# An LSTM expert kernel: state halves exchanged by label, so that one half alone takes the input

## The chip, the cores and the metric

The kernel runs on one core of a Trainium2 chip, as one program. The metric is the device time of an execution in microseconds. Before the change it is 1760.58 us, the median of 3 runs (1759.59 to 1762.61).

## The reference, cut to what matters

A token sequence of 16 x 512 goes through an embedding with a short-time spectrum, local attention, and a layer of eight LSTM experts of which each token takes two. The experts' layer is this (from the reference, cut):

```
logits = flat_x @ router_w + router_b
top_vals, top_idx = jax.lax.top_k(logits, K)
rw = jax.nn.softmax(top_vals, axis=1)
mask = (top_idx.T[:, None, :] == jnp.arange(E)[None, :, None]).astype(x.dtype)
expert_x = (mask[..., None] * flat_x[None, None]).reshape(K, E, S_, B_, I_)
...
gates = xt @ Wi + h @ Wh + b
i_, f_, g_, o_ = jnp.split(gates, 4, axis=-1)
c = jax.nn.sigmoid(f_) * c + jax.nn.sigmoid(i_) * jnp.tanh(g_)
h = jax.nn.sigmoid(o_) * jnp.tanh(c)
...
y = jnp.einsum('ken,nk,keno->no', mask, rw, out)
```

E is 8 experts, K is 2 choices. The scan runs over 16 steps, with 512 columns (sequence positions) in each. For each choice k and expert e there is a state of its own (h and c, 128 x 512), which goes on in every step; its input is x where the k-th choice is e, and zero elsewhere. So an expert has two states, 128 x 1024 together, and at most one of the two gets an input at a given column, since the two choices of a token differ.

## The kernel before, in words

All tensors have the 128 features on the partitions and the columns along the free dimension. The program is written out for five engines by hand, with semaphores. The unit of time in the code is t, from 0 to 31 in a step: t = 4 e + g, with the expert e (a unit) and the gate g in the order I, G, F, O. Each engine's function `step(s, ...)` walks over t and issues what belongs there. `run_front` issues beside it the front of the next step (embedding, norms, attention, choice of experts), each piece at the t that the tables PE_AT, ACT_AT, DVE_AT and SP_AT give for it; pieces for the step after begin at t = 24. Nothing is reordered at run time: an instruction that waits holds its engine's queue.

One unit, on each engine:

- TensorE, `unit_gate` (line 551): for each gate, twelve f16 products of 512 columns into one of two PSUM slots. An f32 operand is held as two f16 parts, HI and LO; three products (HI HI, HI LO, LO HI) stand for one. There are two halves k (the two choices), and an input and a recurrent part: 3 x 2 x 2. Gate n waits until the tanh of gate n-2 has emptied its slot. At g = 0 also `unit_y` (L557), one f32 product of the chosen state of unit e-2 with wo.
- Scalar: `gate_tanh` (L713, 1024 columns) for each gate into `tmp`, `cell_tanh` (L720) at g = 3, `split_hi` (L724, the HI part of h of the unit before) at g = 0.
- VectorE: `hidden` of the unit before at g = 0 (L1051); at g = 1 `masked_input` of the next unit (L1044, both halves, both parts), `hidden_lo` (L1056) and `input_part` (L1066); at g = 2 `chosen` of the unit before (L1087 selects the half that the token chose, L1091 multiplies by the weight) and `cell` (L1072, L1076). Step 0 has no gate F and L1063 in place of L1066.
- SyncE loads masks for unit e+2 at g = 1 and the weight rows at g = 3, each broadcast to 128 partitions from a small DRAM tensor.

Pieces of the front that the prediction names: L841 one-hot rows, L463 embedding, L851 and L981 variance, L857 normalisation (first at t = 29, second at t = 19), L1163 root on GpSimd, L470 and L643 transpose and copy xnT (t = 30), L475 the q, k, v products (t = 31), L490 window scores, L502 values (t = 15), L516 transposes of the second normalised input (t = 20), L817 residuals of the weights ahead of step 0.

## Time and profile before

| | before |
|---|---|
| median of 3 runs | 1760.58 us |
| profiled execution | 1761.26 us |
| its span | 1759.5 us |
| TensorE busy (matmul) | 1692.6 us, 96% |
| VectorE busy | 1543.5 us, 88% |
| Scalar busy | 1000.6 us, 57% |
| GpSimd busy | 48.8 us, 3% |
| granted TensorE clock, mean | 0.986 of full speed |

The span is the time from the first to the last instruction of the profiled execution. The first 90 us hold the set-up and the first front; steps of some 106 us follow. Times in the rows are counted from the span's start.

### The profile page before, as it was taken

The numbers are of one execution on the slowest core, as the hardware profiler recorded it, in microseconds if no ns is written. First come the engines' busy times: TensorE is split into PE (matmuls) and PEld (weight loads), VectorE is DVE, ScalarE is ACT, GpSimd is POOL, SyncE is SP. The second block draws the span as 40 slices with busy tenths as digits, with TensorE's granted clock in tenths as the row PEclk, the third lists the DMA queues.
The fourth block names the chain that finished last, engine by engine and source line by source line (L and its number), as shares of the span: only waits on it lengthen the run. The fifth ranks groups of instructions, "written<-read, shape, count | busy, mean of one in ns | idle before, by whom it ended". The sixth has DMA issues, their size and how long they took to land.

```text
span 1759.5 us, 25844 instructions
## 1 busy us (share of the span) xinstructions
PE 1692.6 (96%) x9864; PEld 822.0 (47%) x9864; DVE 1543.5 (88%) x2419; ACT 1000.6 (57%) x1124; POOL 48.8 (3%) x42
## 2 busy tenths in 40 slices
PE   6776999999999999999999999999999999999998
PEld 3333444444544444444444544444444444544443
DVE  5788898989989899898989989899898989989865
ACT  4165566565565655656565565656556565565543
POOL 1000000000000000000000000000000000000000
PEclk8898999999999999999999999999999999999999
DMA  4132313313232232313214232232423224132220
GB/s 135 33 73 62 84 44 70 68 44 77 61 71 48 66 69 47 75 53 68 66 47 78 53 77 50 56 78 48 72 55 63 63 55 79 45 78 58 60 63 29
DMA packets 204092, 110.96 MB, mean 63 GB/s; under 512 B 125796, under 2 KB 185111, under 8 KB 203968
## 3 DMA queue, kind: packets, MB, share of 16 engines
q1 hardware_dynamic: 203888, 109.28, 27.8%
q8 instruction: 78, 1.28, 0.3%
q14 instruction: 46, 0.38, 0.1%
q10 hardware_dynamic: 80, 0.02, 0.0%
HBM read 89.84 MB, written 4.74 MB: 54 GB/s over the span
## 4 chain that ended last, share of the span: by engine, by line
PE 52%; DVE 33%; issue 9%; ACT 3%; DMA 1%; SPq 1%; POOL 0%; DVEq 0%; ACTq 0%; POOLq 0%
PE gates L551 40%; DVE tmp L1072 4%; PE yp L557 3%; DVE Hs L1056 3%; DVE xm L1044 3%; DVE C L1076 3%; DVE tmp L1087 2%; DVE tmp L1051 2%; DVE tmp L1066 2%; PE FA L490 2%; PE FA L475 1%; DVE z L1091 1%; ACT tmp L713 1%; DVE xn L857 1%; PE FB L463 1%
## 5 line engine op out<-in xcount | busy, mean ns | idle before, releaser
L713 ACT ACTIVATE tmp<-gates,bias_sb 128x1024 f32<-128x1024 f32 x504 | 558.6, 1109 | 444.0 <-PE gates L551 442.9
L551 PE MATMUL gates<-xm,wi_sb 128*128 128x512 f16 x3024 | 738.0, 380 | 5.3 <-ACT tmp L713 5.3
L551 PE MATMUL gates<-Hs,wh_sb 128*128 128x512 f16 x2880 | 699.9, 379 | 0.0
L551 PEld LDWEIGHTS gates<-xm,wi_sb 128*128 128x128 f16 x3024 | 291.7, 98 | 391.5 <-issue 90.8
L551 PEld LDWEIGHTS gates<-Hs,wh_sb 128*128 128x128 f16 x2880 | 281.8, 98 | 339.8
L720 ACT ACTIVATE tmp<-C 128x1024 f32<-128x1024 f32 x128 | 135.3, 1057 | 176.3 <-DVE C L1076 171.1
L1051 DVE SCALAR_TENSOR_TENSOR tmp<-tmp 128x1024 f32<-128x1024 f32 x128 | 156.5, 1222 | 42.8 <-ACT tmp L720 41.0
L1066 DVE SCALAR_TENSOR_TENSOR tmp<-tmp 128x1024 f32<-128x1024 f32 x120 | 145.4, 1212 | 51.5 <-ACT tmp L713 51.5
L1056 DVE SCALAR_TENSOR_TENSOR Hs<-tmp,Hs 128x1024 f16<-128x1024 f32 x120 | 147.0, 1225 | 15.2 <-ACT Hs L724 15.2
L1044 DVE TENSOR_TENSOR xm<-xs,masks 128x2048 f16<-128x2048 f16 x128 | 156.1, 1219 | 2.8 <-DMA masks<-mask_scratch 2.8
L1076 DVE SCALAR_TENSOR_TENSOR C<-tmp 128x1024 f32<-128x1024 f32 x120 | 147.0, 1225 | 4.1
L724 ACT ACTIVATE Hs<-tmp 128x1024 f16<-128x1024 f32 x120 | 126.7, 1056 | 38.8 <-DVE tmp L1051 38.8
L1072 DVE SCALAR_TENSOR_TENSOR tmp<-tmp,C 128x1024 f32<-128x1024 f32 x120 | 145.7, 1214 | 0.6
L557 PE MATMUL yp<-z,wo_sb 128*128 128x512 f32 x256 | 134.5, 607 | 8.8 <-DVE z L1091 8.8
L1091 DVE TENSOR_TENSOR z<-tmp,roww 128x512 f32<-128x512 f32 x128 | 88.6, 692 | 13.6 <-DVE tmp L1087 0.5
L1087 DVE COPY_PREDICATED tmp<-rowk,tmp 128x512 f32<-128x512 uint16 x128 | 93.4, 729 | 0.1
L1163 POOL TENSOR_TENSOR rstd<-veps,mhalf 128x4 f32<-128x4 f32 x32 | 45.2, 1414 | 1556.6 <-DVE veps L981 1152.1
L557 PEld LDWEIGHTS yp<-z,wo_sb 128*128 128x128 f32 x256 | 47.8, 193 | 38.9 <-issue 11.9
L502 PE MATMUL FA<-vwin,diag 128*128 128x32 f16 x1344 | 36.2, 177 | 5.6 <-DVE vwin L941 5.6
L490 PEld LDWEIGHTS FA<-xn,diag 128*128 128x128 f16 x1344 | 38.0, 97 | 7.8 <-issue 5.1
L596 PE MATMUL yp<-identb 128*128 128x512 bf16 x127 | 37.5, 457 | 3.4 <-DVE bias_sb L807 3.4
L502 PEld LDWEIGHTS FA<-vwin,diag 128*128 128x128 f16 x1344 | 35.9, 97 | 9.9 <-DVE vwin L941 6.6
(162 smaller groups left out, 1194.3 us busy)
## 6 DMA issues: line engine op xcount, KB each, us to landing
masks<-mask_scratch SPq DMA_DIRECT2D x128, 256.0 KB, 5.3
roww<-mw_scratch SPq DMA_DIRECT2D x128, 256.0 KB, 3.6
rowk<-mask_scratch SPq DMA_DIRECT2D x128, 128.0 KB, 2.9
...
out_dram<-h SPq DMA_DIRECT2D x16, 256.0 KB, 2.3
...
```

Of the source, the lines that this page charges most:

```text
L551: last = mm(gates[:, slot, k * SEQ:(k + 1) * SEQ], w, v, start=(i < K), stop=(i >= len(seq) - K))
L557: mm(yp[:, :], wo_sb[:, e, :], z32[:, :], start=False, stop=(e == E - 1)).then_inc(s_y, 1)
L713: A(tmp[:, gate_at(gate, e), :], gates[:, (n - 1) % 2, :], ACT.Tanh, bias=bias_sb[:, e, gate:gate + 1], scale=UNSCALE).then_inc(s_tanh, 1)
L720: A(tmp[:, TANH_C, :], C[:, e, :], ACT.Tanh, scale=0.5).then_inc(s_tc, 1)
L724: A(Hs[:, e, HI, :], tmp[:, gate_at(O, e), :], ACT.Copy, scale=V_SCALE).then_inc(s_hhi, 1)
L1044: TT(xm[:, e % 2, :, :, :], xv, mv_, ALU.mult).then_inc(s_xm, 1)
L1051: STT(out=at, in0=at, scalar=1.0, in1=tmp[:, TANH_C, :], op0=ALU.add, op1=ALU.mult).then_inc(s_h, 1)
L1056: STT(out=Hs[:, e, LO, :], in0=tmp[:, gate_at(O, e), :], scalar=V_SCALE, in1=Hs[:, e, HI, :], op0=ALU.mult, op1=ALU.subtract).then_inc(s_h ...
L1066: STT(out=at_i, in0=at_i, scalar=1.0, in1=at_g, op0=ALU.add, op1=ALU.mult).then_inc(s_u, 1)
L1072: STT(out=at_f, in0=at_f, scalar=1.0, in1=C[:, e, :], op0=ALU.add, op1=ALU.mult).then_inc(s_v, 1)
L1076: STT(out=C[:, e, :], in0=at_f, scalar=0.5, in1=tmp[:, gate_at(I, e), :], op0=ALU.mult, op1=ALU.add).then_inc(s_c, 1)
L1087: V.copy_predicated(at[:, 0:SEQ], rowk1[:, e % 2, :].bitcast(u16), at[:, SEQ:2 * SEQ]).then_inc(s_sel, 1)
```

## The change

The two halves of an expert's state are no longer tied to choice 1 and choice 2. Half 0 is the half that is fed at this step. A label (`lab`) per token position and expert tells which of the two states stands in half 0; where the state that is to be fed stands in half 1, the mask `mk_swap` is set, and h and c exchange their halves at these columns, before the unit's gates are computed. `mk_sel` is 1 where the expert is chosen at all.

- The input products run on half 0 alone: three f16 products of 512 columns. `xm` has half its size.
- wh and h are kept in f32: one f32 product of 512 columns for each half, in place of six f16 ones. `Hs`, `split_hi` and `hidden_lo` are gone. In the first step one f16 product of a zeroed tile clears half 1.
- The exchange: Scalar writes a copy of c (`copy_c`, at g = 1 for the next unit) and of h (`copy_h`, at g = 2 for the unit after the next) with the halves swapped, two instructions of 512 columns each, into the single buffers `Cx` and `Hx`. VectorE copies them back under the mask, 1024 columns each: `swap_h` at g = 1 for the next unit, `swap_c` at g = 3 for the next unit. For unit 0 of the next step they stand at t = 30 and 31. TensorE's first gate of a unit waits for `swap_h`, `cell` for `swap_c`, each copy for the swap before it.
- `chosen` reads half 0, so L1087 and the rowk load go. The output gate's buffer in `tmp` is single. The mask load of a unit waits also for the swaps of the unit two before it.
- The choice of experts computes `mk_sel`, `mk_swap` and the new `lab`: five small instructions in place of three. Ahead of step 0, wh is scaled in place by Scalar, and the three residuals of wh on VectorE go.

```
@@ -81,17 +81,18 @@
         wi_sb = sb("wi_sb", [P, E, 2, 4 * P], f16)
-        wh_sb = sb("wh_sb", [P, E, 2, 4 * P], f16)
+        wh_sb = sb("wh_sb", [P, E, 4 * P])
         wo_sb = sb("wo_sb", [P, E, P])
         bias_sb = sb("bias_sb", [P, E, 4])
         C = sb("C", [P, E, K * SEQ])
-        Hs = sb("Hs", [P, E, 2, K * SEQ], f16)
-        tmp = sb("tmp", [P, 7, K * SEQ])
-        masks = sb("masks", [P, 2, K, SEQ], f16)
-        xm = sb("xm", [P, 2, K, 2, SEQ], f16)
+        H = sb("H", [P, E, K * SEQ])
+        Cx = sb("Cx", [P, K * SEQ])
+        Hx = sb("Hx", [P, K * SEQ])
+        tmp = sb("tmp", [P, 6, K * SEQ])
+        masks = sb("masks", [P, 2, 2, SEQ], f16)
+        xm = sb("xm", [P, 2, 2, SEQ], f16)
         xs = sb("xs", [P, 2, 2, SEQ], f16)
         h2 = sb("h2", [P, 2, TILES, D])
-        rowk1 = sb("rowk1", [P, 2, SEQ], f16)
         roww = sb("roww", [P, 2, SEQ])
         z32 = sb("z32", [P, SEQ])
...
@@ -363,6 +368,10 @@
                     sp.wait_ge(S["mout"], (s + 1) * 16)
                 if e >= 2 or not is_zero(s):
                     sp.wait_ge(s_xm, s * E + e - 1)
+                swapped = (s - 1) * E + e - 1
+                if swapped > 0:
+                    sp.wait_ge(s_h_swap, swapped)
+                    sp.wait_ge(s_c_swap, swapped)
                 sp.wait_ge(s_enc_out, 32)
                 src = mask_dram[bass.ds(s, 1), :, :].rearrange("a (k e) t -> (a k) e t", k=K)[:, e, :]
                 sp.dma_start(masks[:, e % 2, :, :], src.rearrange("(a k) t -> a k t", a=1)
...
@@ -538,17 +545,17 @@
                 if g == 0:
                     pe.wait_ge(s_xm, s * E + e + 1)
                     if not first:
-                        pe.wait_ge(s_hlo, s * E + e - E + 1)
-                parts = [(wi_sb, lambda k, v: xm[:, e % 2, k, v, :])]
-                if not first:
-                    parts.append((wh_sb, lambda k, v: Hs[:, e, v, k * SEQ:(k + 1) * SEQ]))
-                seq = []
-                for w, mov in parts:
-                    for wpart, vpart in ((HI, HI), (HI, LO), (LO, HI)):
-                        for k in range(K):
-                            seq.append((w[:, e, wpart, gate * P:(gate + 1) * P], mov(k, vpart), k))
-                for i, (w, v, k) in enumerate(seq):
-                    last = mm(gates[:, slot, k * SEQ:(k + 1) * SEQ], w, v, start=(i < K), stop=(i >= len(seq) - K))
+                        pe.wait_ge(s_h_swap, s * E + e - E + 1)
+                rows_of = slice(gate * P, (gate + 1) * P)
+                fed, other = gates[:, slot, 0:SEQ], gates[:, slot, SEQ:2 * SEQ]
+                for wpart, vpart in ((HI, HI), (HI, LO), (LO, HI)):
+                    mm(fed, wi_sb[:, e, wpart, rows_of], xm[:, e % 2, vpart, :], start=(wpart == HI and vpart == HI),
+                       stop=(first and wpart == LO))
+                if first:
+                    last = mm(other, wi_sb[:, e, HI, rows_of], zero_in, start=True, stop=True)
+                else:
+                    mm(fed, wh_sb[:, e, rows_of], H[:, e, 0:SEQ], start=False, stop=True)
+                    last = mm(other, wh_sb[:, e, rows_of], H[:, e, SEQ:2 * SEQ], start=True, stop=True)
                 last.then_inc(s_gate, 1)
             def unit_y(s, e):
...
@@ -706,8 +714,8 @@
                 m = s * E + e
                 if gate == F and m >= 1:
                     act.wait_ge(s_h, m)
-                elif gate == O and m >= 2:
-                    act.wait_ge(s_z, m - 1)
+                elif gate == O and m >= 1:
+                    act.wait_ge(s_h, m)
                 elif m >= 2:
                     act.wait_ge(s_c, m - 1)
                 A(tmp[:, gate_at(gate, e), :], gates[:, (n - 1) % 2, :], ACT.Tanh, bias=bias_sb[:, e, gate:gate + 1],
...
@@ -719,9 +727,22 @@
                     act.wait_ge(s_h, e)
                 A(tmp[:, TANH_C, :], C[:, e, :], ACT.Tanh, scale=0.5).then_inc(s_tc, 1)
-            def split_hi(s, e):
-                act.wait_ge(s_h, s * E + e + 1)
-                A(Hs[:, e, HI, :], tmp[:, gate_at(O, e), :], ACT.Copy, scale=V_SCALE).then_inc(s_hhi, 1)
+            def copy_c(s, e):
+
+                n = (s - 1) * E + e
+                if n:
+                    act.wait_ge(s_c_swap, n)
+                for k in range(K):
+                    A(Cx[:, k * SEQ:(k + 1) * SEQ], C[:, e, (1 - k) * SEQ:(2 - k) * SEQ], ACT.Copy).then_inc(s_c_copy, 1)
+
+            def copy_h(s, e):
+
+                n = (s - 1) * E + e
+                act.wait_ge(s_h, n + 1)
+                if n:
+                    act.wait_ge(s_h_swap, n)
+                for k in range(K):
+                    A(Hx[:, k * SEQ:(k + 1) * SEQ], H[:, e, (1 - k) * SEQ:(2 - k) * SEQ], ACT.Copy).then_inc(s_h_copy, 1)
             def y_out(s):
                 act.wait_ge(s_y, (s + 1) * E)
...
@@ -734,24 +755,34 @@
                         gate_tanh(s, e, g, first)
                     if t == YT_AT and not first:
                         y_out(s - 1)
-                    if g == 0 and e and not last:
-                        split_hi(s, e - 1)
-                    elif g == 0 and not e and not first:
-                        split_hi(s - 1, E - 1)
                     if g == 3:
                         cell_tanh(s, e)
+                    if g == 1 and e < E - 1 and not first:
+                        copy_c(s, e + 1)
+                    elif g == 1 and e == E - 1 and not last:
+                        copy_c(s + 1, 0)
+                    if g == 2 and e < E - 2 and not first:
+                        copy_h(s, e + 2)
+                    elif g == 2 and e >= E - 2 and not last:
+                        copy_h(s + 1, e + 2 - E)
                     run_front(front, t, s)
...
@@ -1026,10 +1054,17 @@
                     wait("k2", b1)
                     TT(IX, K1, Mb(8), ALU.mult).then_inc(S["wa"], 1)
                     TT(IX2, K2, Mb(9), ALU.mult).then_inc(S["wb"], 1)
-                    V.tensor_copy(mk[:, :, 0:E], K1)
-                    V.tensor_copy(mk[:, :, E:2 * E], K2)
+                    TT(mk_sel, K1, K2, ALU.add).then_inc(S["sel"], 1)
+                    if not is_zero(b):
+                        wait("sw_", b)
+                    TT(EQ, lab[:, :, :], K2, ALU.not_equal).then_inc(S["ne"], 1)
                     wait("wb", b1)
-                    TT(mw[:, :, :], IX, IX2, ALU.add).then_inc(S["mwc"], 1)
+                    TT(mw[:, :, :], IX, IX2, ALU.add)
+                    wait("sel", b1)
+                    wait("ne", b1)
+                    TT(mk_swap, EQ, mk_sel, ALU.mult).then_inc(S["mwc"], 1)
+                    wait("mwc", b1)
+                    TT(lab[:, :, :], lab[:, :, :], mk_swap, ALU.not_equal).then_inc(S["sw_"], 1)
             def masked_input(s, e, par, xfirst):
...
@@ -1039,22 +1074,31 @@
                 if not xfirst:
                     n = s * E + e - 2
                     dve.wait_ge(s_gate, gates_to(n // E, n % E, NG - 1))
-                xv = xs[:, par, :, :].rearrange("p (a v) t -> p a v t", a=1).to_broadcast([P, K, 2, SEQ])
-                mv_ = masks[:, e % 2, :, :].rearrange("p k (a t) -> p k a t", a=1).to_broadcast([P, K, 2, SEQ])
-                TT(xm[:, e % 2, :, :, :], xv, mv_, ALU.mult).then_inc(s_xm, 1)
+                mv_ = masks[:, e % 2, 0:1, :].to_broadcast([P, 2, SEQ])
+                TT(xm[:, e % 2, :, :], xs[:, par, :, :], mv_, ALU.mult).then_inc(s_xm, 1)
+
+            halves = lambda ap: ap.rearrange("p (k t) -> p k t", k=K)
+
+            def swap_h(s, e):
+
+                n = (s - 1) * E + e
+                dve.wait_ge(s_h_copy, K * (n + 1))
+                V.copy_predicated(halves(H[:, e, :]), masks[:, e % 2, 1:2, :].to_broadcast([P, K, SEQ]).bitcast(u16),
+                                  halves(Hx[:, :])).then_inc(s_h_swap, 1)
+
+            def swap_c(s, e):
+
+                n = (s - 1) * E + e
+                dve.wait_ge(s_c_copy, K * (n + 1))
+                V.copy_predicated(halves(C[:, e, :]), masks[:, e % 2, 1:2, :].to_broadcast([P, K, SEQ]).bitcast(u16),
+                                  halves(Cx[:, :])).then_inc(s_c_swap, 1)
             def hidden(s, e):
                 dve.wait_ge(s_tc, s * E + e + 1)
                 dve.wait_ge(s_tanh, gates_to(s, e, 3))
-                at = tmp[:, gate_at(O, e), :]
-                STT(out=at, in0=at, scalar=1.0, in1=tmp[:, TANH_C, :],
+                STT(out=H[:, e, :], in0=tmp[:, gate_at(O, e), :], scalar=1.0, in1=tmp[:, TANH_C, :],
                     op0=ALU.add, op1=ALU.mult).then_inc(s_h, 1)
-
-            def hidden_lo(s, e):
-                dve.wait_ge(s_hhi, s * E + e + 1)
-                STT(out=Hs[:, e, LO, :], in0=tmp[:, gate_at(O, e), :], scalar=V_SCALE, in1=Hs[:, e, HI, :],
-                    op0=ALU.mult, op1=ALU.subtract).then_inc(s_hlo, 1)
             def input_part(s, e, first):
                 dve.wait_ge(s_tanh, gates_to(s, e, 1))
...
@@ -1068,6 +1112,7 @@
             def cell(s, e):
                 dve.wait_ge(s_tanh, gates_to(s, e, 2))
+                dve.wait_ge(s_c_swap, s * E + e - E + 1)
                 at_f = tmp[:, gate_at(F, e), :]
                 STT(out=at_f, in0=at_f, scalar=1.0, in1=C[:, e, :],
                     op0=ALU.add, op1=ALU.mult).then_inc(s_v, 1)
...
@@ -1078,17 +1123,11 @@
             def chosen(s, e):
                 n = s * E + e
-                dve.wait_ge(s_row_in[e % 2], 32 * (s * (E // 2) + e // 2 + 1))
-                if s < STEPS - 1:
-                    dve.wait_ge(s_hlo, n + 1)
-                else:
-                    dve.wait_ge(s_h, n + 1)
-                at = tmp[:, gate_at(O, e), :]
-                V.copy_predicated(at[:, 0:SEQ], rowk1[:, e % 2, :].bitcast(u16), at[:, SEQ:2 * SEQ]).then_inc(s_sel, 1)
+                dve.wait_ge(s_row_in[e % 2], 16 * (s * (E // 2) + e // 2 + 1))
+                dve.wait_ge(s_h, n + 1)
                 if n:
                     dve.wait_ge(s_y, n)
-                dve.wait_ge(s_sel, n + 1)
-                TT(z32[:, :], at[:, 0:SEQ], roww[:, e % 2, :], ALU.mult).then_inc(s_z, 1)
+                TT(z32[:, :], H[:, e, 0:SEQ], roww[:, e % 2, :], ALU.mult).then_inc(s_z, 1)
             def add_y(s, par):
                 dve.wait_ge(s_yback, s + 1)
...
@@ -1106,12 +1145,15 @@
                         hidden(s - 1, E - 1)
                     if g == 1 and e < E - 1:
                         masked_input(s, e + 1, par, first and e == 0)
-                    if g == 1 and e and not last:
-                        hidden_lo(s, e - 1)
-                    elif g == 1 and not e and not first:
-                        hidden_lo(s - 1, E - 1)
+                    if g == 1 and e < E - 1 and not first:
+                        swap_h(s, e + 1)
                     if t == XM_AT and not last:
                         masked_input(s + 1, 0, 1 - par, False)
+                        swap_h(s + 1, 0)
+                    if g == 3 and e < E - 1 and not first:
+                        swap_c(s, e + 1)
+                    elif g == 3 and e == E - 1 and not last:
+                        swap_c(s + 1, 0)
                     if g == 2 and e:
                         chosen(s, e - 1)
                     elif g == 2 and not first:
```

## Rows read from the trace of the kernel before

**Rows 1.** Stretches: us, then each engine's busy us (instructions), clock, DMA share, GB/s.
```profile
91.09:177.26 86.17, 59.86 (x373) 28.18 (x372) 73.93 (x131) 50.90 (x60) 2.01 (x2) 0.90 0.29 69
918.49:1024.37 105.88, 105.20 (x621) 51.39 (x620) 96.89 (x151) 62.54 (x71) 2.92 (x2) 1.00 0.29 62
940.44:988.17 47.73, 47.11 (x281) 22.32 (x279) 46.72 (x69) 25.64 (x27) 1.91 (x1) 1.00 0.33 70
```

**Rows 2.** Timeline of TensorE: start, us, engine, line, operation, tiles, count, [idle before].
```profile
81.46 1.16 PE L463 MATMUL FB<-table,rows 41*128 41x128 f32 x8 [2.06 <-DVE rows L841]
...
909.01 1.46 PE L551 MATMUL gates<-Hs,wh_sb 128*128 128x512 f16 x6
910.30 1.46 PE L551 MATMUL gates<-xm,wi_sb 128*128 128x512 f16 x6
...
915.92 1.88 PE L475 MATMUL FA<-xnT,wqkv_sb 128*128 128x512 f32 x4
...
918.49 1.46 PE L551 MATMUL gates<-xm,wi_sb 128*128 128x512 f16 x6
...
988.23 0.66 PE L516 MATMUL FB<-ident,xn 128*128 128x128 f32 x4 [0.52 <-DVE xn L857]
```

**Rows 3.** Timeline of VectorE, same columns, in the first front and a middle step.
```profile
76.26 4.56 DVE L817 SCALAR_TENSOR_TENSOR wh_sb<-C,wh_sb 128x2048 f16<-128x2048 f32 x3
...
940.44 1.23 DVE L1066 SCALAR_TENSOR_TENSOR tmp<-tmp 128x1024 f32<-128x1024 f32 x1 [1.58 <-ACT tmp L713]
941.59 0.73 DVE L1087 COPY_PREDICATED tmp<-rowk,tmp 128x512 f32<-128x512 uint16 x1
942.42 0.69 DVE L1091 TENSOR_TENSOR z<-tmp,roww 128x512 f32<-128x512 f32 x1
...
1013.99 0.17 DVE L851 TENSOR_SCALAR veps<-mv 128x4 f32<-128x4 f32 x1
1015.02 1.23 DVE L1056 SCALAR_TENSOR_TENSOR Hs<-tmp,Hs 128x1024 f16<-128x1024 f32 x1 [0.86 <-ACT Hs L724]
1016.17 1.11 DVE L857 TENSOR_SCALAR xn<-h_sb,mv,rstd 128x128 f32<-128x128 f32 x4
```

**Rows 4.** Waits: who waited for whom: us in total, times, longest; then Scalar's timeline.
```profile
PE FB L516 <- DVE xn L857: 11.6, 16, 2.5
...
975.04 1.06 ACT L720 ACTIVATE tmp<-C 128x1024 f32<-128x1024 f32 x1 [4.24 <-DVE C L1076]
```

**Rows 5.** Groups of instructions (mean ns after the busy us), and the DMA issue of masks.
```profile
L1056 DVE SCALAR_TENSOR_TENSOR Hs<-tmp,Hs 128x1024 f16<-128x1024 f32 x120 | 147.0, 1225 | 15.2 <-ACT Hs L724 15.2
L1091 DVE TENSOR_TENSOR z<-tmp,roww 128x512 f32<-128x512 f32 x128 | 88.6, 692 | 13.6 <-DVE tmp L1087 0.5
L1087 DVE COPY_PREDICATED tmp<-rowk,tmp 128x512 f32<-128x512 uint16 x128 | 93.4, 729 | 0.1
L669 ACT ACTIVATE ew<-vf 128x464 f16<-128x464 f32 x16 | 11.8, 739 | 0.0
L672 ACT ACTIVATE ew<-prod 128x512 f32<-128x512 f32 x16 | 9.8, 614 | 2.6 <-DVE prod L890 2.6
...
masks<-mask_scratch SPq DMA_DIRECT2D x128, 256.0 KB, 5.3
```

**Rows 6.** TensorE in step 0: timeline, then stretches (us, busy, clock, DMA share, GB/s).
```profile
129.36 2.32 PE L502 MATMUL FA<-vwin,diag 128*128 128x32 f16 x84 [3.05 <-DVE vwin L941]
131.52 2.72 PE L551 MATMUL gates<-xm,wi_sb 128*128 128x512 f16 x6
...
146.20 0.65 PE L516 MATMUL FB<-ident,xn 128*128 128x128 f32 x4 [2.52 <-DVE xn L857]
...
130.92:134.33 3.41, 3.41 (x36) 0.50 0.22 73
159.60:163.72 4.12, 0.03 (x2) 0.75 0.04 12
165.05:168.46 3.41, 3.41 (x11) 0.50 0.73 209
```

More of the change, by code:

```diff
@@ L215, in lm_tower_kernel @@
         s_whi = sem("s_whi")
+        s_wh = sem("s_wh")
+        s_hzero = sem("s_hzero")
+        s_c_copy = sem("s_c_copy")
+        s_h_copy = sem("s_h_copy")
+        s_c_swap = sem("s_c_swap")
+        s_h_swap = sem("s_h_swap")
         s_wlo = sem("s_wlo")
@@ L320, in _ @@
             load(enc_dram[P:NBJ, :], encB, s_enc_out)
-            load(wh_st.rearrange("p a (b n) -> p (a b) n", b=2), wh.rearrange("e i n -> i e n"), s_wh_load)
+            load(wh_sb[:, :, :], wh.rearrange("e i n -> i e n"), s_wh_load)
             load(wo_sb[:, :, :], wo.rearrange("e i n -> i e n"), s_wo_load)
@@ L424, in _ @@
             zeros = xnT[:, :].bitcast(f16)
+            zero_in = H[:, E - 1, 0:SEQ // 2].bitcast(f16)
             pe.wait_ge(s_warm, 1)
@@ L765, in _ @@
                 if t == ACT_AT["h"]:
[L766 removed]
+                    split_wi_hi()
                 if t == ACT_AT["summary"]:
[L768 removed]
+                    scale_wh()
             def step_p(s, par, first, last):
@@ L807, in _, with split_wi_lo @@
             TS(bias_sb[:, :, O:O + 1], bias_sb[:, :, O:O + 1], 0.5, None, ALU.mult).then_inc(s_prep, 1)
-            def split_w_lo(a, b):
-                parts = [(src.rearrange("p a (b n) -> p (a b) n", b=2)[:, :, c0 * P:c1 * P],
-                          dst[:, :, :, c0 * P:c1 * P], W_SCALE * f * half)
-                         for src, dst, f in ((wi_st, wi_sb, 1.0), (wh_st, wh_sb, 0.5))
-                         for c0, c1, half in ((0, 2, 0.5), (2, 3, 1.0), (3, 4, 0.5))]
-                for n, (src, dst, scale) in list(enumerate(parts))[a:b]:
+            def split_wi_lo():
+                v = wi_st.rearrange("p a (b n) -> p (a b) n", b=2)
+                for n, (c0, c1, half) in enumerate(((0, 2, 0.5), (2, 3, 1.0), (3, 4, 0.5))):
                     dve.wait_ge(s_whi, n + 1)
-                    STT(out=dst[:, :, LO, :], in0=src, scalar=scale, in1=dst[:, :, HI, :],
-                        op0=ALU.mult, op1=ALU.subtract).then_inc(s_wlo, 1)
+                    STT(out=wi_sb[:, :, LO, c0 * P:c1 * P], in0=v[:, :, c0 * P:c1 * P], scalar=W_SCALE * half,
+                        in1=wi_sb[:, :, HI, c0 * P:c1 * P], op0=ALU.mult, op1=ALU.subtract).then_inc(s_wlo, 1)
             def wait(name, n):
```

47 lines of the change are left out of this document (22 added, 25 removed).

## The prediction

> **What bounds the kernel now.** I read the table of busy time first. In a middle step of the recurrence, 105.88 us long, TensorE is busy for 105.20 us and VectorE for 96.89 us [rows 1]. The busy total alone doesn't say whether TensorE streams or is held, so I went to its timeline. One gate is twelve f16 products on 512 columns. Six of them take 1.295 us from start to start (909.01 to 910.30, rounded there), 0.216 each, so a gate takes 2.59 us, and in the timeline the next begins at once [rows 2]. TensorE sets the pace, and 32 gates fill 82.9 of the 105.9 us.
>
> VectorE's timeline shows a second bound just under the first. From 940.44 to 988.17 it has no idle time that ends on another engine: 46.72 us busy in 47.73 us [rows 1, 3]. At the end of that stretch TensorE waits for it, 0.52 us, at the transposes of the second normalised input (L516), and the list of waits has 16 such waits, one for each front [rows 2, 4]. Scalar is busy for 62.54 us of the step [rows 1] and once waits 4.24 us for VectorE's cell state [rows 4]. So a faster TensorE soon meets a VectorE that has next to no slack between units 1 and 5 of each step.
>
> **TensorE, per gate.** The change leaves three f16 products (3 x 0.216 = 0.65 us) and adds two f32 products on 512 columns. The price of these is in the trace: three in a row, L475 (two records each: four in the row shown and two behind it), go from 915.92 to 918.49, 2.57 us, so 0.857 us each with their weight loads hidden, and the f16 gate behind them starts without a gap [rows 2]. A gate becomes 0.65 + 1.71 = 2.36 us, which is 0.23 less. If nothing else bound, a step would lose 32 x 0.23 = 7.4 us.
>
> **VectorE, per unit.** What an instruction costs in a full queue is the distance between starts. Removed: the low half of the hidden state (L1056, 1015.02 to 1016.17, 1.15), the selection of the state half (L1087, 941.59 to 942.42, 0.83), and half of the masked input (L1044, 2048 to 1024 elements, about 1.17 to 0.6) [rows 3]. Added: two predicated copies of 1024 elements. The nearest row is the 512-element one, 729 ns; 1024 f32 elements against 512 cost 1225 - 692 = 533 ns more in the two-operand instructions [rows 5]. That gives 1262 ns, of which some 0.08 lies under the next instruction (1225 against 1.15), so 1.18 in the queue, and I count 1.17. Bounds: 0.73 (no growth with size) and 2.33 (growth at twice that slope: 729 - 533 = 196 fixed, 2 x 1066 on top). I take 1.17, since kinds and types are those of L1087. Balance of a unit: +2.34 - 1.15 - 0.83 - 0.57 = -0.2 us. VectorE gets no faster to speak of. Two small instructions more in the choice of experts add 0.4 us a step.
>
> The Trainium skill (VectorE: DVE Perf Modes, section on the TRN2 errata) gives (N+151)/0.96 ns for an fp32 instruction with two tensors; the 692 ns of the 512-element product agree [rows 5]. By it a swap would be an estimated 1224 ns, and the forecast some 4 us lower.
>
> **Scalar, per unit.** Removed: one conversion of 1024 (1056 ns). Added: four copies of 512. No f32 copy of 512 within SBUF is in the trace; nearest is the 512-element exponential there, 614 ns; half of the cell's tanh of 1024 (1.06) gives 0.53 as the lower bound, the strided f16 conversion of 464 (739 ns) the upper [rows 4, 5]. I take 614: 4 x 0.61 - 1.06 = +1.4 us a unit, +11 us a step, 62.5 to 74 of some 102. There is room, if the order permits it. Each pair follows a tanh and is shorter than a gate (2.36 us) together with it: 1.11 + 1.13 less overlap.
>
> **The step, followed along.** T is TensorE's start of the first gate, 918.49. Three pieces.
> (a) T to VectorE's input part of unit 1 (L1066). Before: TensorE ends that gate at 939.10, VectorE starts at 940.44 after 1.58 us of waiting [rows 3]. Six gates are shorter by 0.23 each: 21.95 - 1.37 = T + 20.6. VectorE's own work before it shrinks by 0.8 us (two L1056, one L1087 and two half L1044 gone, three swaps in), so it still arrives first, near T + 19.6.
> (b) From there to the end of the second normalisation (L857). Before 47.73. Four L1087 go (-3.3), three L1056 and three half L1044 go (-5.1), three swaps of h and four of c come (+8.2). The fourth swap of c stands ahead of the normalisation in the queue. Result 47.5, practically unchanged, so T + 68.1.
> TensorE, 21 gates shorter by 0.23, would be there at 69.05 - 4.8 = T + 64.2, a little later for a wait of 0.9 behind the cell's tanh in unit 3. So the 0.5 us wait at L516 becomes about 3 us. The faster gates of units 1 to 5 bring nothing.
> (c) From L516 to the next T: 36.14 before, TensorE's throughout [rows 2]; 11 gates give 33.6. Add 0.9 for a new wait: in unit 7 Scalar's copy of h for the next step waits for VectorE's swap, and behind it stands the copy of xnT that TensorE's q, k, v products need. VectorE comes late there since L1056, which filled the 1.0 us between variance and GpSimd's root (1013.99, 1015.02, 1016.17), is gone [rows 3].
> Sum: 68.1 + 34.5 = 102.6 against 105.88, 3.3 us saved a step, 46 us over steps 1 to 14.
>
> **The ends.** Step 0 lasts 86.17 us and is VectorE's: 73.93 busy there, TensorE 59.86 [rows 1]. Each unit loses 1.15 + 0.83 + 0.57 = 2.5 us; eight give 20, less two swaps 2.3. The 12.2 us that VectorE idles there (86.17 - 73.93), waits for loads, TensorE and Scalar in the front's chain, may grow as it gets shorter. I take 16, bounds 8 and 20. Before it, three residuals of wh on VectorE (4.56 us) go, and with them the 2.06 us that TensorE waits for rows: -2 [rows 3, 2]. The last step has no front, TensorE alone: 32 x 0.23 = 7.4. At the end one L1087: -0.8. The swap waits of the mask loads hold SP's queue, but the swap waited for comes more than a unit ahead of the masks' use, and a load lands in 5.3 us [rows 5]: nothing.
>
> **The clock.** With TensorE idle 3.05 us before L502 the granted clock was 0.50 from 130.92 on, and six products took 2.72 instead of 1.46 us; after a wait of 4.1 us it was 0.50 again; after 2.52 us idle it was 1.00, since four transposes took 0.65 us as at 988.23 (0.66) [rows 6, 2]. In the middle step of before it is 1.00 throughout [rows 1]. A 3 us wait at L516 lies near the edge. A stretch like that of 130.92 (3.41 us at 1.2 GHz instead of 2.4) costs 1.7 us of TensorE's work, and all of it counts in (c). I take it in 6 of 10 steps: 1.0 a step, +14.
> The Trainium skill (TensorE: Matmul & The Clock Gate, section HAM oscillation) has this as its rule against gaps between bursts of matmuls; the trace agrees by the 3.05 and 4.1 us.
>
> **Sum.** 1761.26 (span 1759.5 and 1.8 around it) - 46 - 16 - 2 - 7.4 - 0.8 + 14 = 1703. The profiled execution is 0.7 above the median, so 1702 stands for a median.
>
> **Rivals.** (1) TensorE alone sets the step, because VectorE's lag is absorbed: each of 14 steps loses 7.4 + 0.7, so 1761 - 113 - 26 = 1622. For it: VectorE's 96.9 us fit in 97.8. Against it: the gapless 47.73 us and the 16 waits at L516 [rows 3, 4]. 10%.
> (2) The clock falls in every step and for twice as long: 3.4 instead of 1.0 a step, +34, so 1737. For it: in the 4.1 us wait the clock fell already within the wait (0.75) and still 0.50 two microseconds into the work behind it [rows 6]. 17%.
> (3) Slower than before: the predicated copy of 1024 elements with one mask row for both halves runs at the 2.33 us bound. Seven swaps stand in (b), one in (c). It decides from 58 / (14 x 8) = 0.5 us more than taken, so from 1.8 us each; at 2.33 it is 1.07 x 8 x 14 = 120, so 1822. Only the row of 512 speaks against it. 6%.
> (4) Scalar, VectorE and TensorE form a ring: Scalar holds a tanh back behind a copy that waits for a swap, in each unit some 0.4 us that reach TensorE, 8 x 0.4 x 14 = 45, so 1748. For it: the output gate's tmp is single now and every copy waits for the swap before it. Against it: the copies are due a unit ahead, and VectorE is the one waited for anyway. 10%.
> The forecast has 57%, with its own range 1685 to 1720 (clock never, or always once).
>
> **How the numbers follow.** Range 1650 to 1745: it takes in (2), and leaves out (1), (3) and part of (4), under 2 in 10. A measurement of this kernel tells 0.2% (3.5 us) from nothing. Slower: (3) and a little of (4), 0.07; same 0.03; faster 0.90.
>
> **What would show it.** TensorE: f32 products on wh_sb 0.86 us apart, TensorE's busy share lower than 96%. COPY_PREDICATED with 1024 elements at 1.26 us, x240. A wait at L516's successor near 3 us, 14 times, and the clock at 0.5 after some of them. VectorE without gaps between units 1 and 5. The step near 102.6 to 104. Wrong: steps of 98 (no wait there), swaps over 1.4 us, waits for Scalar's copies in front of the swaps, or a step 0 still above 80 us.

## The result, and the profile after

| | before | after |
|---|---|---|
| median | 1760.1 us (4 runs) | 1701.9 us (1699.0 to 1704.3, 4 runs) |
| profiled execution | 1761.26 us | 1699.02 us |
| its span | 1759.5 us | 1697.2 us |
| TensorE busy | 96% | 93% |
| VectorE busy | 88% | 90% |
| Scalar busy | 57% | 67% |

The ratio is 0.967, with the interval 0.965 to 0.969; 1702 was forecast. First come the stretches of the kernel after, by the columns of [rows 1]: step 0, a whole middle step (T = 884.64), and its three pieces, cut where the forecast cut them.

```profile
88.33:162.94 74.61, 50.89 (x326) 22.95 (x325) 60.31 (x121) 48.72 (x63) 2.01 (x2) 0.89 0.32 70
884.64:987.72 103.08, 98.53 (x461) 47.40 (x460) 96.53 (x154) 71.28 (x95) 2.93 (x2) 1.00 0.26 54
884.64:905.23 20.59, 20.59 (x140) 10.53 (x139) 17.20 (x21) 14.37 (x22) 0.00 (x0) 1.00 0.41 63
905.23:952.96 47.73, 44.03 (x208) 20.30 (x206) 47.13 (x70) 31.91 (x40) 1.92 (x1) 1.00 0.24 54
952.96:987.72 34.76, 33.91 (x115) 16.57 (x116) 32.19 (x64) 25.00 (x34) 1.01 (x1) 1.00 0.21 48
```

The piece in the middle is as long as before to the hundredth (47.73 us), and VectorE is busy for 47.13 of it. TensorE, which had 0.6 us of idle time there, now has 3.7. The clock is 1.00 in all of them but step 0.

TensorE's timeline just ahead of T shows a gate and the last wait of the step:

```profile
873.42 0.81 PE L552 MATMUL gates<-xm,wi_sb 128*128 128x512 f16 x3
874.06 1.02 PE L557 MATMUL gates<-H,wh_sb 128*128 128x512 f32 x2
874.92 1.02 PE L558 MATMUL gates<-H,wh_sb 128*128 128x512 f32 x2
875.78 0.81 PE L552 MATMUL gates<-xm,wi_sb 128*128 128x512 f16 x3
...
881.96 1.98 PE L482 MATMUL FA<-xnT,wqkv_sb 128*128 128x512 f32 x4 [0.85 <-ACT xnT L651]
```

From 873.42 to 875.78 is one gate, 2.36 us. (Two records, L557 and L558, are one f32 product; the pairs start 0.86 us apart.) The list of waits, by total, count and longest, says that what L482 shows once happens in each step, and at four places:

```profile
PE FB L523 <- DVE xn L885: 30.4, 16, 2.4
PE FA L482 <- ACT xnT L651: 15.6, 16, 3.1
PE FA L514 <- DVE attn L990: 12.4, 15, 0.9
PE yp L571 <- DVE h L1136: 12.3, 15, 0.8
```

L523 is the old L516. VectorE's timeline shows what it does ahead of that wait, here with the root on GpSimd set among its rows; VectorE has no gap from 945.48 to 952.82:

```profile
948.12 0.17 DVE L1009 TENSOR_SCALAR veps<-mv 128x4 f32<-128x4 f32 x1
948.20 1.23 DVE L1117 SCALAR_TENSOR_TENSOR tmp<-tmp,C 128x1024 f32<-128x1024 f32 x1
948.37 1.92 POOL L1203 TENSOR_TENSOR rstd<-veps,mhalf 128x4 f32<-128x4 f32 x1 [72.41 <-DVE veps L1009]
949.46 1.23 DVE L1121 SCALAR_TENSOR_TENSOR C<-tmp 128x1024 f32<-128x1024 f32 x1
950.60 1.30 DVE L1093 COPY_PREDICATED C<-masks,Cx 128x1024 f32<-128x1024 uint16 x1
951.80 1.10 DVE L885 TENSOR_SCALAR xn<-h,mv,rstd 128x128 f32<-128x128 f32 x4
```

The variance is ready at 948.29. The normalisation (L885) starts at 951.80, behind the cell's two instructions and the swap of another unit. The root that it also needs ends at 950.29 by GpSimd's record (times on that engine are rough), and the swap starts at 950.60. So of these 3.5 us it is the swap's 1.2 that the order of the queue could save. Of the groups, those of the change:

```profile
L1093 DVE COPY_PREDICATED C<-masks,Cx 128x1024 f32<-128x1024 uint16 x120 | 158.3, 1319 | 0.0
L1086 DVE COPY_PREDICATED H<-masks,Hx 128x1024 f32<-128x1024 uint16 x120 | 156.6, 1305 | 0.0
L745 ACT ACTIVATE Hx<-H 128x512 f32<-128x512 f32 x240 | 137.1, 623 | 15.3 <-DVE H L1086 15.3
```

**Where the 62.2 us came from.** Between the starts of gates in the two profiled executions: the first gate is 2.8 us earlier (91.09 to 88.33); step 0 is 11.6 shorter (86.17 to 74.61); the thirteen steps 1 to 13 are 36.2 shorter (1376.60 to 1340.37, 103.1 each against 105.89); from there to the end it is 11.7 (205.61 to 193.92), in which step 14 has its 2.8 and the last step and the end 8.9.

### The profile page after: what moved, and what is told of

It reads as the page before. It is cut to its first block, busy times and chain, and to the rows that moved or that the text cites. A ratio compares the mean times of both kernels' runs of the same rounds, so it can differ in the third digit from the quotient of the medians.

```text
span 1697.2 us, 21434 instructions
## 1 busy us (share of the span) xinstructions
PE 1578.6 (93%) x7416; PEld 755.3 (45%) x7416; DVE 1525.2 (90%) x2440; ACT 1131.9 (67%) x1484; POOL 49.5 (3%) x43
## 4 chain that ended last, share of the span: by engine, by line
DVE 47%; PE 28%; issue 12%; ACT 3%; POOL 1%; DVEq 0%; ACTq 0%
PE gates L558 7%; PE gates L557 7%; DVE C L1093 6%; DVE tmp L1117 6%; PE gates L552 6%; DVE H L1086 4%; DVE C L1121 4%; DVE tmp L1110 3%; DVE H L1100 3%; DVE z L1130 3%; PE yp L564 2%; ACT tmp L721 2%; PE FA L497 2%; PE FA L482 2%; DVE xm L1078 2%
## 5 line engine op out<-in xcount | busy, mean ns | idle before, releaser
L558 PE MATMUL gates<-H,wh_sb 128*128 128x512 f32 x960 | 490.2, 592 | 0.0
L557 PE MATMUL gates<-H,wh_sb 128*128 128x512 f32 x960 | 490.2, 592 | 0.0
L552 PE MATMUL gates<-xm,wi_sb 128*128 128x512 f16 x1512 | 411.5, 381 | 5.9 <-ACT tmp L721 3.9
L558 PEld LDWEIGHTS gates<-H,wh_sb 128*128 128x128 f32 x960 | 182.4, 190 | 229.6 <-issue 229.6
L552 PEld LDWEIGHTS gates<-xm,wi_sb 128*128 128x128 f16 x1512 | 143.7, 99 | 282.9 <-issue 196.1
L557 PEld LDWEIGHTS gates<-H,wh_sb 128*128 128x128 f32 x960 | 182.3, 190 | 69.1
L1110 DVE SCALAR_TENSOR_TENSOR tmp<-tmp 128x1024 f32<-128x1024 f32 x120 | 144.9, 1208 | 52.0 <-ACT tmp L721 51.6
L1100 DVE SCALAR_TENSOR_TENSOR H<-tmp 128x1024 f32<-128x1024 f32 x128 | 156.0, 1219 | 5.2 <-ACT tmp L728 5.2
L1093 DVE COPY_PREDICATED C<-masks,Cx 128x1024 f32<-128x1024 uint16 x120 | 158.3, 1319 | 0.0
L1086 DVE COPY_PREDICATED H<-masks,Hx 128x1024 f32<-128x1024 uint16 x120 | 156.6, 1305 | 0.0
L1121 DVE SCALAR_TENSOR_TENSOR C<-tmp 128x1024 f32<-128x1024 f32 x120 | 147.0, 1225 | 4.1
L745 ACT ACTIVATE Hx<-H 128x512 f32<-128x512 f32 x240 | 137.1, 623 | 15.3 <-DVE H L1086 15.3
L736 ACT ACTIVATE Cx<-C 128x512 f32<-128x512 f32 x240 | 136.8, 622 | 0.0
L482 PE MATMUL FA<-xnT,wqkv_sb 128*128 128x512 f32 x64 | 32.6, 633 | 15.6 <-ACT xnT L651 15.6
```

Of the source, the lines that this page charges most:

```text
L552: mm(fed, wi_sb[:, e, wpart, rows_of], xm[:, e % 2, vpart, :], start=(wpart == HI and vpart == HI), stop=(first and wpart == LO))
L557: mm(fed, wh_sb[:, e, rows_of], H[:, e, 0:SEQ], start=False, stop=True)
L558: last = mm(other, wh_sb[:, e, rows_of], H[:, e, SEQ:2 * SEQ], start=True, stop=True)
L1086: V.copy_predicated(halves(H[:, e, :]), masks[:, e % 2, 1:2, :].to_broadcast([P, K, SEQ]).bitcast(u16), halves(Hx[:, :])).then_inc(s_h_swa ...
L1093: V.copy_predicated(halves(C[:, e, :]), masks[:, e % 2, 1:2, :].to_broadcast([P, K, SEQ]).bitcast(u16), halves(Cx[:, :])).then_inc(s_c_swa ...
L1100: STT(out=H[:, e, :], in0=tmp[:, gate_at(O, e), :], scalar=1.0, in1=tmp[:, TANH_C, :], op0=ALU.add, op1=ALU.mult).then_inc(s_h, 1)
```

## The experiments

Each edit is one of the kernel after, and its step is the distance between the first gates of two steps in the middle of the run. The intervals of the ratios to before are about 0.002 on either side. Two questions were open: why the step stands at 103.1 us where TensorE's work is 98.5, and what the clock would have done with a longer wait.

| kernel | median us | ratio to before | step us |
|---|---|---|---|
| after | 1701.9 | 0.967 | 103.1 |
| swap of the cell later | 1687.5 | 0.957 | 102.15 |
| Scalar's copy of the state later | 1682.6 | 0.955 | 101.98 |
| both | 1665.3 | 0.945 | 100.80 |
| one input product less, all gates | 1706.4 | 0.968 | 102.9 to 104.9 |
| the same, gates 6 to 20 alone | 1708.3 | 0.971 | 103.1 or 104.8 |
| the same, the other gates | 1685.8 | 0.958 | 101.4 to 103.5 |
| VectorE 0.9 us later | 1732.6 | 0.985 | 105.7 |
| VectorE 1.8 us later | 1759.5 | 0.999 | 106.4 to 108.1 |
| swaps of 2 columns | 1629.1 | 0.926 | 98.22 |
| Scalar's copies of 2 columns | 1687.5 | 0.959 | 102.2 |
| both orders, masked input on GpSimd | 1791.4 | 1.017 | 109.1 |

**1. The swap of the cell behind the normalisation.** The front's piece is issued first at the last gate of a unit.

```
-                    if g == 3 and e < E - 1 and not first:
-                        swap_c(s, e + 1)
-                    elif g == 3 and e == E - 1 and not last:
-                        swap_c(s + 1, 0)
...
                     run_front(front, t, s)
+                    if g == 3 and e < E - 1 and not first:
+                        swap_c(s, e + 1)
+                    elif g == 3 and e == E - 1 and not last:
+                        swap_c(s + 1, 0)
```

> The changed kernel (1702), with swap_c behind the front's piece at g = 3 instead of ahead of it, so that the second normalisation (t = 19) comes one swap earlier in VectorE's queue. Theory A (from TensorE's G gate of unit 1 to the second normalisation VectorE alone sets the step, from there on TensorE): L523 starts 1.2 us earlier after T, the step goes from 103.1 to 101.9, 14 x 1.2 = 17, so 1685. Rival B (TensorE alone sets the step): no change, 1702. Rival C (the order only moves the wait: hidden comes later, Scalar's tanh with it): 1702 or more.

Measured: 1687.5 us, the step 0.95 us shorter. The waits at L514 and L571 are gone from the list, and a new one stands in their place: 1.0 us in each step before a gate of unit 3, behind Scalar's tanh. The wait at L523 stayed (29.6 us), and the one at L482 grew from 15.6 to 19.6, which is from 0.85 to 1.05 in a step. So 1.2 us of VectorE's queue taken from in front of the results that TensorE waits for came out as 0.95 in the step, and the wait at L482 took the rest.

**2. Scalar's copy of the state behind its front piece.** In unit 7 Scalar copied the state (L745, which waits for VectorE's swap) ahead of the transposed input (L651) that TensorE's L482 needs.

```
+                    run_front(front, t, s)
                     if g == 2 and e < E - 2 and not first:
                         copy_h(s, e + 2)
                     elif g == 2 and e >= E - 2 and not last:
                         copy_h(s + 1, e + 2 - E)
-                    run_front(front, t, s)
```

> The changed kernel, with Scalar's copy_h behind the front's piece, so that the copy of xnT (t = 30) doesn't wait for swap_h. Theory A: TensorE's wait of 0.85 us at the q, k, v products goes, the step is 102.3, 14 x 0.85 = 12, so 1690. Rival (something else is late at that point, since VectorE's h and c of unit 7 come then too): under 0.3 a step, 1698 to 1702.

Measured: 1682.6 us, a larger gain than the 1690 expected. The wait at L482 is gone, and the step is 1.1 us shorter. Step 0 gained too: the first gate came later than in the kernel after (92.17 for 88.33 us), and the first gate of step 1 still came earlier (159.49 for 162.94).

**3. Both orders.**

> Both changes of order together. Theory A: the two lie in different pieces of the step and add up: 103.1 - 1.2 - 0.85 = 101.05, so 1702 - 29 = 1673. If one hides the other: 1685.

Measured: 1665.3 us, step 100.80: 2.3 us less than after, against 0.95 + 1.12. The two add up, so they are separate costs, and the 0.2 more is what the wait at L482 had grown by in kernel 1. This kernel computes the whole result and beats both. Its list of waits keeps one of the four, and has the wait in unit 3 of kernel 1 beside it:

```profile
PE FB L523 <- DVE xn L885: 29.3, 16, 2.7
PE gates L552 <- ACT tmp L721: 17.5, 17, 2.0
```

**4. One input product less in every gate.** The product of the low part of the weight with the high part of the input is left out, 0.216 us a gate; this kernel and kernels 5 and 6 leave that product out of the result.

```
-                for wpart, vpart in ((HI, HI), (HI, LO), (LO, HI)):
+                for wpart, vpart in ((HI, HI), (HI, LO)):
...
```

> The changed kernel with the input product of wi's LO part and x's HI part left out (each gate 0.216 us shorter on TensorE, output less exact). Theory A: of the 32 gates of a middle step only the 17 outside VectorE's piece count (6 before it, 11 behind L523): 17 x 0.216 = 3.7 a step, 51 over 14 steps, 7 in the last step, so 1643; the wait at L523 grows by 3.2 in sum with its neighbours. Rival B (TensorE alone): 32 x 0.216 = 6.9 a step, so 1598. Rival D (VectorE alone sets the whole step): nearly 1702. If the wait gets long enough for the clock to fall, 1.7 a step more than A: up to 1667.

Measured: 1706.4 us. With 6.9 us less work for TensorE the step got 0.8 us longer in the mean (103.9 in steps 1 to 13). The waits grew, and the clock fell twice in eleven of these thirteen steps and once in the other two. The list of waits, and one stretch with the clock down, by the columns of [rows 1]:

```profile
PE FB L523 <- DVE xn L885: 39.9, 16, 2.8
PE FA L482 <- ACT xnT L651: 29.7, 16, 4.1
PE FA L514 <- DVE attn L990: 22.8, 15, 1.7
PE yp L571 <- DVE h L1136: 21.6, 15, 1.5
```

```profile
857.10:860.50 3.40, 3.40 (x8) 1.63 (x6) 2.21 (x3) 0.90 (x3) 0.00 (x0) 0.50 0.39 47
```

There the granted clock is 0.50, which is 1.2 GHz instead of 2.4. The number lies next to rival D's ("nearly 1702"), but for another reason: kernel 6 shows that TensorE's work outside VectorE's piece does count. What no expectation had is less work and a clock that falls this often together. Against the kernel after the medians are 0.3% apart, which the scatter of the executions nearly covers, so that the kernel got slower is not shown; that its steps got longer is.

**5 and 6. The same product less by place.** First in gates 6 to 20 of a step alone, between the input part of unit 1 and the second normalisation; then in the 17 others alone.

```
-                for wpart, vpart in ((HI, HI), (HI, LO), (LO, HI)):
+                for wpart, vpart in ((HI, HI), (HI, LO), (LO, HI))[:2 if (6 <= 4 * e + g <= 20) and not first else 3]:
```

> Leaves out the third input product (LO by HI) of the 15 gates 6 to 20 alone, those between the input part and the second normalisation, in steps 1 to 14 and the last: 15 x 0.216 = 3.2 us of TensorE's work in a step. Theory A (there VectorE's chain sets the pace, so TensorE only waits more): 1698 to 1705 us, with the waits of TensorE in a step higher by about 3 us; and more by up to 1.7 us a step (to 1730) if the clock falls in the waits. Rival B (TensorE alone sets the pace): 1702 - 15 x 3.2 = 1654 us.

> Leaves out the third input product (LO by HI) of the 17 gates 0 to 5 and 21 to 31 alone, in steps 1 to 15: 17 x 0.216 = 3.7 us of TensorE's work in a step. Theory A (outside the stretch from the input part to the second normalisation TensorE sets the pace): the step falls from 103.1 to about 99.4 us, in all 1702 - 15 x 3.7 = 1647 us; up to 1660 if VectorE, whose own work in a gate is then as long as TensorE's, takes the pace in part, and up to 1672 if the clock falls once a step. Rival B (VectorE sets the pace through the whole step): 1702 us.

Measured inside: 1708.3 us. Of thirteen steps seven last 103.04 to 103.11 us, the same as after although TensorE has 3.2 us less to do. The other six last 1.6 to 1.7 us longer than the same steps of after. Two steps in a row:

```profile
680.79:783.84 103.05, 96.83 (x446) 46.57 (x445) 96.51 (x154) 71.38 (x95) 2.93 (x2) 0.98 0.26 54
783.84:888.65 104.81, 97.02 (x447) 46.59 (x445) 96.61 (x154) 71.22 (x95) 2.93 (x2) 0.98 0.25 53
```

Both have one stretch of 3.4 us at 1.2 GHz. In the second it begins 70 us into the step, behind L523, where it counts in full. In the first it begins 30 us into it, where TensorE has slack: the steps without such a fall have a wait of 1.23 us at L552, 43.5 us into them, which is missing here, and the step is no longer than in the kernel after. TensorE's timeline there:

```profile
709.40 1.09 PE L571 MATMUL yp<-rows,bo_sb 8*128 8x512 f32 x2 [1.46 <-DVE h L1136]
710.42 1.97 PE L564 MATMUL yp<-z,wo_sb 128*128 128x512 f32 x2
```

A wait of 1.46 us stands before this fall, and behind the next step's same wait (1.46 us, 812.45) the clock stays. It is no single case: of the steps 1 to 14 ten have a fall behind this wait and four have none, and behind the wait at L523, 2.53 us in each of them, seven have one and seven have none.

Measured outside: 1685.8 us, between the two expectations (1647 to 1672, and 1702), and the shortest step 101.43. The step lost 1.7 of the 3.7 us. The wait at L482 took 1.0 a step of the rest (0.85 to 1.87 us), two small new waits for VectorE (at L535 and L470, 0.38 and 0.34 us) took 0.7, and behind the wait at L482 the clock fell in six of thirteen steps (102.8 to 103.5 us). So between the input part and the normalisation TensorE sets nothing, and outside it sets the pace in part only.

**7 and 8. VectorE later by a known time.** One memset of 1024 (kernel 7) or 2048 (kernel 8) f16 elements in front of the second normalisation, 912 and 1765 ns.

```
+                        if at == "xn2" and b > 0:
+                            V.memset(idle[:, :], 1.0)
```

> The changed kernel (step 103.1) with one instruction of no use, about 1.1 us (memset of 1024 elements), in VectorE's queue ahead of the second normalisation in every front but the first. Theory A: VectorE's piece sets the step up to there, so each of the steps 0 to 14 grows by 1.1, +16, 1718. If TensorE's wait before L523, now about 3 us, makes the granted clock fall, up to 1.7 us a step more, 1742. Rival (VectorE has room there): 1702.

> The same with an instruction of twice the length, about 2.2 us; TensorE's wait before L523 is about 4 us. Theory A with the full clock: +33, 1735. With the clock at half speed for 3.4 us in every step: + 24 more, 1759. Rival: 1702.

Measured: 1732.6 and 1759.5 us. The first is the cleaner. Here are its wait and what comes behind it (line numbers are one higher there, so L524 is L523):

```profile
969.17 0.65 PE L524 MATMUL FB<-ident,xn 128*128 128x128 f32 x4 [2.79 <-DVE xn L888]
...
970.31 1.88 PE L558 MATMUL gates<-H,wh_sb 128*128 128x512 f32 x2
971.98 1.91 PE L559 MATMUL gates<-H,wh_sb 128*128 128x512 f32 x2
```

The wait is 2.79 us instead of 1.88. The f32 products behind it take 1.7 us from start to start instead of 0.86. Two steps in a row, one with a fall and one of the two without:

```profile
1110.49:1216.15 105.66, 100.23 (x461) 48.12 (x460) 97.32 (x155) 71.28 (x95) 2.92 (x2) 0.98 0.26 52
1216.15:1320.15 104.00, 98.55 (x461) 47.41 (x460) 97.36 (x155) 71.26 (x95) 2.93 (x2) 1.00 0.28 53
```

0.9 us on VectorE cost 0.9 us (103.1 to 104.00), and the clock added 1.7 in 12 of 14 steps. The step without a fall had the same wait (2.78 us). With 1.8 us of delay the wait was up to 3.9 us, and the step 106.4 to 108.1: the clock fell in every step, in some for twice 3.4 us. That nearly took back the whole gain of the change.

**9. Both swaps cut to 2 columns of a half.** The exchange is left out but for these.

```
-                V.copy_predicated(halves(H[:, e, :]), masks[:, e % 2, 1:2, :].to_broadcast([P, K, SEQ]).bitcast(u16),
-                                  halves(Hx[:, :])).then_inc(s_h_swap, 1)
+                V.copy_predicated(halves(H[:, e, :])[:, :, 0:2], masks[:, e % 2, 1:2, 0:2].to_broadcast([P, K, 2]).bitcast(u16),
+                                  halves(Hx[:, :])[:, :, 0:2]).then_inc(s_h_swap, 1)
...
```

> The changed kernel with both swaps on 2 columns of each half instead of 512 (the exchange is left out but for these), 1.3 us to under 0.1 each; Scalar's copies and all waits stay. Theory A: VectorE has 2.3 us a unit less, the waits of TensorE go, a step is TensorE's 105.9 - 7.4 - 0.7 = 97.8 and a little for Scalar, 14 x 5.2 = 73, step 0 loses 2: about 1628. Rival (Scalar's copies hold the units): over 1680.

Measured: 1629.1 us, step 98.22. The wait at L523 fell to 5.9 us in 16, and TensorE is the bound:

```profile
PE 1573.1 (97%) x7416; PEld 759.1 (47%) x7416; DVE 1268.2 (78%) x2440; ACT 1130.2 (70%) x1484; POOL 49.4 (3%) x43
```

**10. Scalar's copies cut to 2 columns.** The exchange then takes stale halves. (Not shown: both buffers are zeroed once at the start.)

```
-                    A(Cx[:, k * SEQ:(k + 1) * SEQ], C[:, e, (1 - k) * SEQ:(2 - k) * SEQ], ACT.Copy).then_inc(s_c_copy, 1)
+                    A(Cx[:, k * SEQ:k * SEQ + 2], C[:, e, (1 - k) * SEQ:(1 - k) * SEQ + 2], ACT.Copy).then_inc(s_c_copy, 1)
...
```

> The changed kernel with Scalar's copies on 2 columns of each half instead of 512 (the exchange then brings in stale data); swaps and waits stay. Theory A: Scalar's copies cost nothing but 0.8 us a step ahead of xnT, so the step is 102.3 and the time 1690; since the order alone (copy behind xnT) gave 1683, 1683 to 1690. Rival (ring of Scalar, VectorE and TensorE, in each unit): at least 3 us a step, under 1660.

Measured: 1687.5 us, step 102.2. The wait at L482 is gone; those at L523, L514 and L571 stand at 28.8, 12.4 and 11.9 us, as in after. So the length of Scalar's copies costs the step that one wait and no more.

**11. Masked input on GpSimd, with both orders.** Try to give VectorE less to do: 8 x 682 ns a step.

```
-                TT(xm[:, e % 2, :, :], xs[:, par, :, :], mv_, ALU.mult).then_inc(s_xm, 1)
+                G_.tensor_tensor(xm[:, e % 2, :, :], xs[:, par, :, :], mv_, ALU.mult).then_inc(s_xm, 1)
...
```

> The masked inputs of the steps (L1078, 682 ns of VectorE each, 8 in a step) go to GpSimd, beside the two moved orders (swap of the cell behind the front piece, copy for the state behind the transposed front on Scalar), which together gave 1665.3 us and 100.80 us a step. Theory A (what is left in a step is VectorE's path from the input part to the second normalisation): three to four masked inputs lie in that piece, so the step loses 1.8 to 2.5 us, to 98.3 to 99.0, where TensorE alone (98.2 us with the swaps cut to 2 columns) stops it: 1630 to 1642 us. Rival B: GpSimd is slower at the masked input than VectorE and either holds up the input product or lengthens VectorE's own instructions beside it; then 1665 us or more.

Measured: 1791.4 us, slower than before (1.017, interval 1.015 to 1.019) and 8.3 us a step more than kernel 3. Up to 1.7 of these are the clock, which fell once in every step. VectorE is busy for 101.72 us of a step (935.65 to 1044.63), where kernel 3 has 96.43, though it has 5.5 us of products less to do. GpSimd's and VectorE's timelines, set together:

```profile
908.64 3.08 POOL L1200 TENSOR_TENSOR xm<-xs,masks 128x1024 f16<-128x1024 f16 x1 [11.30 <-PE gates L558]
...
908.53 1.22 DVE L1107 SCALAR_TENSOR_TENSOR tmp<-tmp,C 128x1024 f32<-128x1024 f32 x1
909.78 3.02 DVE L1111 SCALAR_TENSOR_TENSOR C<-tmp 128x1024 f32<-128x1024 f32 x1
...
921.15 1.23 DVE L1111 SCALAR_TENSOR_TENSOR C<-tmp 128x1024 f32<-128x1024 f32 x1
```

L1111 takes 3.02 us beside GpSimd's product and 1.23 alone: it ends 1.08 us after GpSimd's end at 911.72, as if it had begun there. Over the run its mean is 1646 ns against 1225 for the same line of after (L1121), and GpSimd's product takes 2667 ns where VectorE's took 682. The Trainium skill (SBUF — State Buffer, section "SBUF: two separate sides") says that VectorE with two SBUF inputs and GpSimd reading SBUF hold a shared port pair in turn, each for a whole instruction; the 3.02 us agree. So does the row before: L1107 had started first and took its usual 1.22 us, and from its end (909.75) to GpSimd's there are 1.97 us, near the shortest of GpSimd's products (2.12).

## Why the prediction was right, and where its sizes were off

**TensorE's gate.** 2.36 us as worked out. The price of the f32 product, read from three q, k, v products of the kernel before, held to the hundredth.

**Swaps.** Taken at 1.17 us in the queue, measured 1.20 (950.60 to 951.80); 1305 to 1319 ns busy against the 1262 from [rows 5]. The slope of the two-operand instructions was the right neighbour. Rival (3), decided from 1.8 us, is refuted by that. Its bound of 2.33 us was worked out wrong: with twice the slope from the row of 729 ns it is 729 + 1066, so 1.80 us, which only just reaches what that rival needed.

**Scalar's copies.** Taken at 614 ns, measured 622. Scalar is busy for 71.28 us of the step, with 74 forecast. Rival (4), the ring through Scalar, is refuted by kernel 10: without the copies' length only the wait at L482 goes, 1748 us had needed 0.4 us in each unit.

**The three pieces.** (a) T + 20.6 forecast, 20.59 measured. (b) T + 68.1 forecast, 68.32 measured. (c) 34.5 forecast, 34.76 measured, with the new wait behind Scalar's copy at 0.85 for 0.9; kernel 2 shows its cause by taking it away. The step is 103.1 for 102.6; over fourteen steps these 0.5 us are the 7 by which -46 came out as -39. That VectorE holds (b) is shown by kernel 5 (less work for TensorE there shortens no step; seven stay as they were, six are longer by the clock), by kernel 7 (0.9 us more for VectorE is 0.9 in the step) and by kernel 9. Rival (1), TensorE alone, is refuted by the 103.1, and its size was sound: with the swaps gone the step is 98.22 and the whole 1629, near its 1622.

**The waits of (b).** Forecast were 0.9 us in unit 3 and 3 us at the second normalisation, 3.9 together. The three waits are 0.84, 0.83 and 1.88 us, 3.55 together. The total was nearly right. That it would fall on one place was not: TensorE meets VectorE's lag first where it needs the residual (L571) and the attention's sum (L514), both VectorE's results ahead of the normalisation. I had followed VectorE's chain to its end only, and not the results on its way. The wait in unit 3 is real where these two are gone: in kernels 1 and 3 it is 1.0 us, and the one at L523 1.8, with the swap out of the way.

**The clock.** This is the term that was wrong: +14 us forecast, from a fall in 6 of 10 steps, and 0 measured; the clock is 1.00 in every step from 1 to 14. What failed is the edge near 3 us. It was read from two waits of step 0, and the same trace had others. TensorE's timeline in step 0 of the kernel before, and a stretch of it by the columns of [rows 1]:

```profile
100.28 0.56 PE L484 MATMUL FA<-bandb,identb 128*128 128x448 bf16 x1 [2.54 <-DMA diag<-pr]
...
110.06 1.74 PE L557 MATMUL yp<-z,wo_sb 128*128 128x512 f32 x2 [1.45 <-DVE z L1091]
```

```profile
110.44:113.85 3.41, 3.41 (x8) 0.91 (x6) 3.38 (x6) 1.95 (x2) 0.00 (x0) 0.50 0.57 150
```

Behind 1.45 us the clock stood at 0.50, as it did from 100.20 on beside the wait of 2.54, and behind the 2.52 us at 146.20 it did not. The agreement by the 3.05 and 4.1 us that the prediction notes holds for the two waits that it took, and not for these. Kernels 5 and 7 say the same of the steps: the clock fell behind 2.79 us in 12 of 14 steps, and behind 1.46 us in ten of 14. So it was not shown that the fall stayed away because the wait at L523 is 1.88 us and not 3; that the four waits of the kernel after never brought one in this execution is what is measured. Its other three executions took 2.6 to 5.3 us more at a mean clock of 0.985, 0.985 and 0.981 against 0.989, and where they lost it can't be seen. (With the swaps cut, kernel 9, the clock scatters as far, from 0.981 to 0.992, with no wait above 0.25 us in the steps.) The price of a fall, 1.7 us, was right as taken from [rows 6]. Rival (2) is the clock's part of kernel 8: beyond 103.1 and the 2.0 us by which its wait at L523 grew, its steps took 1.3 to 3.0 us more, where the rival had 3.4.

**The ends.** The start gave -2.8 for -2, which shows nothing: in ten kernels with the same code ahead of the first gate it comes at 86.9 to 92.3 us. The last step and the end gave -8.9 for -8.2. Step 0 gave 11.6 and not 16 (it lasts 74.61 us, and 74.20 and 73.96 in kernels 5 and 6, which are the same there): VectorE, busy for 73.93 us of it before, is busy for 60.31 after, 13.6 less where I had counted 17.7, and its idle time grew from 12.2 to 14.3. Two slips in the count explain part of it: seven of the eight removed L1056 and L1087 lie in the stretch, not eight, and I took the 0.83 us between starts for an L1087, which is busy for 0.73 [rows 5]. By busy time the lines that went and came give 8.56 + 5.12 + 4.28 - 2.58 = 15.4. Where in step 0 TensorE waits in the kernel after:

```profile
153.93 0.65 PE L477 MATMUL FB<-ident,xn 128*128 128x128 f32 x4 [3.13 <-DVE xn L885]
...
158.59 2.84 PE L482 MATMUL FA<-xnT,wqkv_sb 128*128 128x512 f32 x4 [3.14 <-ACT xnT L651]
```

The second is the wait of (c), which I had priced for the steps and not for step 0. Without it (kernel 2) step 0 ends at 159.49 us instead of 162.94. How the 4.4 us divide among these was not told apart.

**Why 1702 was met so closely.** Errors cancelled: the clock's 14 us that did not come, against 7 in the steps and 4.4 in step 0, less 1.5 at the two ends. With the clock term at nothing my sum would have been 1689 for the profiled execution, which took 1699.0: 10 too low. Most of the other 4 come from the executions: the profiled one was taken to lie 0.7 above the median and lies 2.9 below. The direction and the bound were understood; the last per cent was luck.
